# A ring of four groups of copied expert rows, and GpSimd's waits by two groups, in the expert stage of a decoder kernel

## The chip, the cores and the metric

The kernel runs on one core of a Trainium2 chip. The metric is the device time of one execution in microseconds (us); lower is better. The whole program is one launch.

## The reference

The reference is a decoder of two layers on 8 sequences of 256 tokens with 256 features, all in float32. Layer 0 has a butterfly state mixing, a cross attention on 64 context tokens and a ternary feed-forward block; layer 1 has a causal self attention, a rotary attention of 16 heads over context and sequence, and a mixture of 32 masked experts. The change lies in this last block alone:

```python
def _L1_ffn_ref(x, weight, scale, expert_masks, router_w):
    logits = jnp.einsum('bsd,ed->bse', x, router_w)
    probs = jax.nn.softmax(logits, axis=-1)
    top1_w = jnp.max(probs, axis=-1)
    top1_idx = jnp.argmax(probs, axis=-1)
    w_scaled = jnp.clip(jnp.round(weight / 0.5), -1.0, 1.0) * scale[:, None]
    def body(out, inputs):
        e_idx, mask_e = inputs
        y = jnp.einsum('bsi,oi->bso', x, w_scaled * mask_e)
        sel = (top1_idx == e_idx)[..., None]
        return jnp.where(sel, y * top1_w[..., None], out), None
...
x = x + _L1_ffn_ref(_layernorm(x, axis=-1), ...)
```

Each token goes through one expert, a 256x256 matrix of ternary values under the expert's mask.

## The kernel before

The kernel writes its waits and the order of every engine's instructions by hand: each engine has one block of code, and semaphores join them. The expert stage is the last one, after the rotary attention.

Tokens are sorted by expert. GpSimd scatters the rows of all 2048 tokens to `tokens_dram`, by 16 indirect DMAs (L1406), so that each tile of 32 rows (`HT`) holds tokens of one expert. There are 96 tiles in 12 groups (`GROUPS`) of 8 tiles (`QT`); two times 128 rows make one group, and `t` counts these halves. For each group u:

- SyncE loads its 256 rows into `sIN`, a ring of eight (`HELD`), at L1214. The load of group u waits, from u = 8 on, until group u - 8 has been stored.
- ScalarE normalizes the rows (`normal`, L1846, two instructions), and after TensorE has transposed them (L2496, four transposes) copies the transposed rows out of PSUM (`turned`, L1855) into `sXT`.
- The rows of the eight experts that the group needs are copied, from the bf16 table `EW` into float32 rows in `sE`, each 128x512: five by VectorE (`staged`, L1096, a cast) and three by ScalarE (`staged`, L1868). Which expert it is comes from a register that is loaded from `f_exu`. `sE` has two buffers, for even and odd groups, in the space of the weights `wq` and `wo`, which are no longer needed. The copy for group u waits on `f_y` until TensorE is through group u - 2.
- TensorE multiplies (`apply`, 32 matmuls in L1887), group u after the transposes of group u + 1 in its order.
- VectorE scales each half by the token's weight and the experts' scale (`scaled`, L1104) and adds the token's own row (`summed`, L1112, for group 0 by halves; `summed_both`, L1119, for the others) into `sY`, a ring of four (`RING`). `summed_both` waits until the store of group u - 4 has landed.
- GpSimd stores each half to `out` by one indirect DMA (L1431), which scatters the rows to the tokens' places.

VectorE's and ScalarE's order in the stage is fixed as follows. VectorE: copies of groups 0 and 1, the two halves of group 0 scaled and summed, copies of group 2, and then for each u from 1 on: scale u, copies of u + 2, sum u. ScalarE: copies of groups 0 and 1, `normal(0)`, `turned(0)`, `normal(1)`, and then for each u from 0 on: `turned(u + 1)`, `normal(u + 2)`, copies of u + 2. TensorE: transposes of u, then `apply(u - 1)`. GpSimd's order is the groups', and it waits once for each group (for group 0 once for each half).

Of the kernel before, what the change touches and what calls it, by code (L numbers as in the profile page):

```python
# [5 lines left out]
B, S, D = 8, 256, 256  # L6
P = 128
J, C = S // P, D // P
# [17 lines left out]
HS = P // HT  # L26
QT = 2 * HS
EARLY = 5
RING = 4
GROUPS = 12  # L30
# [16 lines left out]
def decoder_kernel(nc, I, out, rows, results):  # L47
    F32, BF, U8, U32 = mybir.dt.float32, mybir.dt.bfloat16, mybir.dt.uint8, mybir.dt.uint32
    ALU, ACT, AX = mybir.AluOpType, mybir.ActivationFunctionType, mybir.AxisListType
    ds = bass.ds  # L50

    with ExitStack() as ctx:
# [82 lines left out]
        def cut(at, shape, dt=F32, src=arena):  # L135
            n = 1
            for s in shape:
                n *= s
            words = n if dt == F32 else n // 2
            v = src[:, at:at + words]  # L140
            if dt != F32:
                v = v.bitcast(dt)
            if len(shape) > 1:
                names = "abcd"[:len(shape)]
                v = v.rearrange(f"p ({' '.join(names)}) -> p {' '.join(names)}",
                                **dict(zip(names[1:], shape[1:])))
            return v
# [64 lines left out]
        def held(eng, s, value):  # L212

            eng.wait_ge(s, value)
            eng.sem_inc(s_held, 1)
# [69 lines left out]
        def after(eng, s, value):  # L285

            if type(value) is not int or value > 0:
# [68 lines left out]

        sIN = cut(0, (HELD, 2, DW)); sXN = cut(4160, (RING, 2, D))
        sXT = cut(0, (RING, 2 * C * P), F32, early2)
        sE = [cut(0, (QT, C * D), F32, wide) for wide in (wq[:, :, :].rearrange("p c n -> p (c n)"),
                                                           wo[:, :, :].rearrange("p h d -> p (h d)"))]  # L360
        sT = cut(0, (RING, 2, D), F32, early); sY = cut(2048, (RING, 2, D), F32, early)
        fSLOT = cut(7232, (TOK, NE)); tilesB = cut(7744, (P,)); past = cut(7872, (TILES,)); fBASE = cut(7968, (2, NE))
        fNEWER = cut(8032, (J, NE)); fSHIFT = cut(8096, (NE,)); past2 = cut(8128, (TILES,)); tilesB2 = cut(8224, (P,))
# [27 lines left out]
        def _(dve):  # L391
# [697 lines left out]
            def staged(u):  # L1089

                dve.load(registers, f_exu[0:1, QT * u:QT * u + EARLY])
                if u >= 2:
                    held(dve, f_y, 2 * (u - 1))
                for t in range(EARLY):
                    expert = bass.RuntimeValue.of_register_unchecked(registers[t], min_val=0, max_val=NE - 1)
                    last = dve.tensor_copy(sE[u % 2][:, t, :], EW[:, ds(expert, 1), :].rearrange("p a n -> p (a n)"))  # L1096
                last.then_inc(f_ev, 1)

            def scaled(u, t):
# [18 lines left out]
                dve.wait_ge(f_sc, 2 * u + 2)  # L1118
                dve.tensor_tensor(sY[:, k], sT[:, k], sIN[:, u % HELD, :, 0:D], ALU.add).then_inc(f_yo, 2)  # L1119

            staged(0)
            staged(1)
            for t in range(2):
                scaled(0, t)
                summed(0, t)
            staged(2)
            for u in range(1, GROUPS):
                for t in range(2):
                    scaled(u, t)
                if u + 2 < GROUPS:  # L1130
                    staged(u + 2)
                summed_both(u)


# [82 lines left out]
        def _(pool):  # L1217
# [207 lines left out]
            for u in range(GROUPS):  # L1425
                k = u % RING
                for t in range(2):
                    if u == 0 or t == 0:
                        pool.wait_ge(f_yo, t + 1 if u == 0 else 2 * u + 2)
                    to = sIN[:, u % HELD, t, ID:ID + 1].bitcast(U32)  # L1430
                    pool.indirect_dma_start(out_rows[:, :], bass.IndirectOffsetOnAxis(ap=to, axis=0), sY[:, k, t, :], None,  # L1431
                                            bounds_check=B * S - 1, oob_is_err=False).then_inc(s_stored[k], 16)
# [5 lines left out]
        def _(act):  # L1438
# [422 lines left out]
            def staged(u):  # L1861

                act.load(registers, f_exu[0:1, QT * u + EARLY:QT * u + QT])
                if u >= 2:
                    held(act, f_y, 2 * (u - 1))
                for t in range(EARLY, QT):
                    expert = bass.RuntimeValue.of_register_unchecked(registers[t - EARLY], min_val=0, max_val=NE - 1)
                    last = act.activation(sE[u % 2][:, t, :], EW[:, ds(expert, 1), :].rearrange("p a n -> p (a n)"), ACT.Copy)  # L1868
                last.then_inc(f_ea, 1)

            staged(0)
            staged(1)
            normal(0)
            turned(0)
            normal(1)
            for u in range(GROUPS):
                if u + 1 < GROUPS:
                    turned(u + 1)
                if u + 2 < GROUPS:
                    normal(u + 2)  # L1880
                    staged(u + 2)


        @block.tensor
        def _(pe):
# [588 lines left out]
            def apply(u):  # L2474

                k = u % RING
                after(pe, f_sc, 2 if u == RING - 1 else 2 * (u - RING + 1))
                pe.wait_ge(f_ev, u + 1)
                pe.wait_ge(f_ea, u + 1)
                pe.wait_ge(f_xt, u + 1)  # L2480
                for t in range(2):
                    for c in range(C):
                        for h in range(HS):
                            first = (C * t + c) * P + h * HT
                            last = product(PS[h * HT:(h + 1) * HT, result_bank(u, t), t * D:(t + 1) * D], sXT[:, k, first:first + HT],
                                           sE[u % 2][:, HS * t + h, c * D:(c + 1) * D], c == 0, c == C - 1)
                    last.then_inc(f_y, 1)

            for u in range(GROUPS + 1):
# [64 lines left out]
```

## Time and profile before

| | us |
|---|---|
| median of 3 runs | 1120.06 |
| lowest and highest of them | 1119.53, 1125.9 |
| the profiled execution's own time | 1122.36 |
| its span, from first to last instruction | 1119.6 |
| mean granted TensorE clock over the span | 0.954 |

The span is what the profile's positions count in: a position of 1100 means 1100 us after the first instruction. The expert stage's copies begin at 1059.87 of it, so that the stage takes the last 60 us. The profiled execution's time is 2.76 us over its span. In the rows, PE is TensorE, DVE VectorE, ACT ScalarE, POOL GpSimd, SP SyncE; a q behind the name is the engine's queue, where DMAs are issued. A row of the timeline gives start, duration, engine, line, operation, what is written and read, and in square brackets how long the engine had been idle before it and what ended this.

### The profile page before, as it was taken

Reading aid. Unit: us, or ns where it says so; the run is one execution under the profiler, and the core shown is the slowest. Engines: PE = TensorE matmul, PEld = TensorE weight load, DVE = VectorE, ACT = ScalarE, POOL = GpSimd, SP = SyncE. Lnnn points to the kernel's source line nnn. Section 1 sums busy time; section 2 is a strip of 40 time slices with the busy share of each in tenths; the row PEclk is TensorE's granted clock in tenths of the full one; section 3 lists DMA queues with packets and bytes.
Section 4 is the critical chain, followed back from the end, with each engine's and each line's share of the span. In section 5 each row is a group of like instructions: output and inputs, shape, how many; then the busy total and the mean of one; then the engine's idle time right before and its main releaser. Section 6 shows DMA issues by size and latency. Waiting matters only on the chain.

```text
span 1119.6 us, 21113 instructions
## 1 busy us (share of the span) xinstructions
PE 992.0 (89%) x5879; PEld 679.0 (61%) x5887; DVE 829.7 (74%) x2532; ACT 687.0 (61%) x2310; POOL 314.5 (28%) x516
## 2 busy tenths in 40 slices
PE   7888896899999769899999999999999999968474
PEld 5674454576766435566767767667677676745342
DVE  5768875788888758878878878887788788753365
ACT  2678884776767626656665675576556756741283
POOL 3334322222223312223223222222332222101546
PEclk9789999999999979999999999999999999998687
DMA  9801002212111004000000000000000000000631
GB/s 272 296 1 38 1 0 58 58 58 56 56 56 58 19 1 129 1 16 1 1 15 1 1 16 1 15 2 1 15 1 1 15 0 6 10 1 5 233 118 63
DMA packets 36379, 47.45 MB, mean 42 GB/s; under 512 B 4659, under 2 KB 27067, under 8 KB 36032
## 3 DMA queue, kind: packets, MB, share of 16 engines
q1 hardware_dynamic: 34048, 42.04, 12.5%
q0 software_dynamic: 1920, 4.23, 1.0%
q8 instruction: 34, 0.56, 0.2%
q14 instruction: 57, 0.47, 0.1%
q10 hardware_dynamic: 320, 0.15, 0.0%
HBM read 31.65 MB, written 12.66 MB: 40 GB/s over the span
## 4 chain that ended last, share of the span: by engine, by line
PE 47%; ACT 4%; issue 3%; POOL 3%; DVE 1%; DMA 0%; ACTq 0%; POOLq 0%; DVEq 0%
PE PS L1887 40%; PE PS L2287 3%; PE PS L2267 2%; POOL out_dram L1431 2%; ACT arena L1727 1%; POOL tokens_dram L1406 1%; ACT arena L1735 1%; PE PS L2141 1%; PE PS L2289 0%; ACT causal L1759 0%; PE PS L2496 0%; ACT early L1648 0%; DMA arena<-tokens_dram 0%; PE PS L1897 0%; PE PS L2332 0%
## 5 line engine op out<-in xcount | busy, mean ns | idle before, releaser
L1887 PE MATMUL PS<-early,arena 128*32 128x128 f32 (+6 forms) x920 | 114.5, 353 | 25.0 <-DVE early L711 11.2
L1887 PE MATMUL PS<-wo,early 128*128 128x256 f32 (+1 forms) x704 | 127.7, 385 | 7.8 <-DVE sinT L912 6.4
L1343 POOL TENSOR_SCALAR small<-small 128x4 f32<-128x4 f32 x64 | 17.4, 272 | 409.9 <-ACT mask L1711 236.2
L1887 PE MATMUL PS<-EW,arena 128*128 128x256 f32 (+7 forms) x512 | 116.8, 351 | 11.3 <-DVE small L861 8.4
L1887 PE MATMUL PS<-wq,EW 128*128 128x512 f32 x256 | 124.2, 608 | 1.8 <-DVE arena L837 1.8
L1887 PEld LDWEIGHTS PS<-wo,early 128*128 128x128 f32 (+1 forms) x704 | 105.0, 171 | 32.6 <-issue 9.6
L1727 ACT ACTIVATE arena<-arena,small 128x128 f32<-128x128 f32 (+3 forms) x256 | 119.7, 480 | 4.1 <-DVE small L866 4.1
L1718 ACT ACTIVATE arena<-PS 128x512 f32<-128x512 f32 x64 | 38.6, 603 | 123.8 <-PE PS L2267 123.8
L1887 PEld LDWEIGHTS PS<-EW,arena 128*128 128x128 f32 x512 | 84.2, 192 | 41.9 <-issue 33.2
L861 DVE CUSTOM_DVE_ANT_0 arena<-PS,kmask 128x128 f32<-128x128 f32 (+3 forms) x256 | 91.6, 388 | 22.2 <-PE PS L1887 16.5
L1887 PEld LDWEIGHTS PS<-early,arena 128*32 128x32 f32 (+4 forms) x928 | 58.9, 118 | 74.7 <-issue 34.0
L1711 ACT ACTIVATE mask<-PS 128x128 f32<-128x128 f32 x256 | 67.3, 284 | 45.5 <-PE PS L1887 45.3
L789 DVE TENSOR_REDUCE small<-PS 128x2 f32<-128x256 f32 (+1 forms) x128 | 62.3, 548 | 34.3 <-PE PS L1887 33.5
L1887 PEld LDWEIGHTS PS<-wq,EW 128*128 128x128 f32 x256 | 46.1, 194 | 48.7 <-issue 46.0
L873 DVE TENSOR_SCALAR arena<-arena,small 128x128 f32<-128x128 f32 (+3 forms) x256 | 68.8, 332 | 2.3
L1345 POOL TENSOR_TENSOR small<-small,halves 128x4 f32<-128x4 f32 x64 | 67.3, 1052 | 5.3
L1743 ACT ACTIVATE early<-PS 128x512 f32<-128x512 f32 x64 | 38.1, 595 | 48.7 <-PE PS L1887 48.7
L1887 PE MATMUL PS<-arena,EW 128*128 128x512 f32 (+1 forms) x160 | 64.8, 520 | 2.5 <-ACT arena L1735 2.5
L1691 ACT ACTIVATE arena<-PS,small 128x256 f32<-128x256 f32 x128 | 62.6, 489 | 0.0
L1641 ACT ACTIVATE early<-PS 128x384 f32<-128x384 f32 x64 | 28.0, 488 | 53.1 <-PE PS L2168 53.1
L1735 ACT ACTIVATE arena<-PS 128x512 f32<-128x512 f32 x96 | 54.0, 600 | 5.6 <-PE PS L2289 3.6
L1711 ACT ACTIVATION_READ_ACCUMULATOR mask<-PS 128x1 f32 x256 | 55.2, 216 | 0.0
(341 smaller groups left out, 2316.0 us busy)
## 6 DMA issues: line engine op xcount, KB each, us to landing
EW<-in_masksT_dram SPq DMA_DIRECT2D x32, 256.0 KB, 3.5
experts_dram<-EW SPq DMA_DIRECT2D x32, 128.0 KB, 3.3
EW<-experts_dram SPq DMA_DIRECT2D x4, 1024.0 KB, 10.8
tokens_dram<-EW SPq DMA_DIRECT2D x1, 3120.0 KB, 12.9
arena<-tokens_dram SPq DMA_DIRECT2D x12, 260.0 KB, 4.2
X<-in_x_dram SPq DMA_DIRECT2D x8, 256.0 KB, 4.6
wq<-in_wq_dram SPq DMA_DIRECT2D x1, 2048.0 KB, 10.0
wo<-in_wo_dram SPq DMA_DIRECT2D x1, 2048.0 KB, 17.0
```

What stands on the lines that cost most here:

```text
L789: last = dve.tensor_reduce(d_neg[:, i % 2, j, r:r + 2], PS[:, r:r + 2, at:at + n], AX.X, ALU.max, negate=True)
L861: dve.tensor_tensor_reduce(probs(i, t), PS[:, 3 + t % 2, 0:n], kmask[:, at:at + n], 1.0, LOWEST, ALU.add, ALU.max, e_max[:, t:t + 1]).then ...
L873: last = dve.tensor_scalar(probs(i, t), probs(i, t), e_inv[:, t:t + 1], None, ALU.mult)
L1345: pool.tensor_tensor(e_rqs[:, i % 2, :], e_q3[:, i % 2, :], halves[:, 0:GH], ALU.pow).then_inc(e_rq, 1)
L1691: act.activation(dP[:, i % 2, r, P:3 * P], PS[:, r, P:3 * P], ACT.Exp, bias=d_neg[:, i % 2, 1, r:r + 1], accum_out=d_sum[:, m, 1, r, e:e + ...
L1711: last = act.activation(eSQ[:, h * XD:(h + 1) * XD], PS[:, 1, h * XD:(h + 1) * XD], ACT.Square, accum_out=e_q2[:, i % 2, h:h + 1])
L1718: act.activation(eQT.rearrange("p (t h q) -> p h t q", t=4, h=GH), PS[:, 2, :].rearrange("p (h t q) -> p h t q", t=4, h=GH), ACT.Copy).the ...
L1727: last = act.activation(tile, tile, ACT.Exp, bias=e_neg[:, i % 2, t:t + 1], accum_out=e_sum[:, i % 2, t:t + 1])
L1735: last = act.activation(ePT[:, 512 * k:512 * k + 512], PS[:, 5 + k, :], ACT.Copy)
L1743: act.activation(eOT[:, GH * g:GH * g + GH, j * P:(j + 1) * P].rearrange("p h (t q) -> p h t q", t=4), PS[:, 0, :].rearrange("p (t h q) -> ...
L1887: return pe.matmul(dst, lhs, rhs, start=first, stop=last)
L2287: pe.transpose(PS[:, 5 + k, t * P:(t + 1) * P], eP[:, i % 4, at:at + P], ident[:, :])
```

## The change

`sE` gets four buffers in the place of two. Each is now a list of eight rows of 512 floats, which may lie apart: buffers 0 and 1 lie in `wq` and `wo` as before, buffer 2 in `wk`, `wv`, `wkc`, `wvc`, buffer 3 in `w_in`, `w_out` and the upper half of `early2`; all of these are dead in this stage. The copies for group u wait for group u - 4 instead of u - 2.

Both copying engines copy groups 0 to 3 before anything else of the stage. VectorE then does for each u from 1 on: copies of u + 3, scale u, sum u. ScalarE does for u = 0: `turned(1)`, `normal(2)`; and from u = 1 on: `turned(u + 1)`, `normal(u + 2)`, copies of u + 3.

GpSimd no longer waits for each group: before group 2 it waits for the sums of groups 2 and 3, before group 4 for 4 and 5, and so on to 8 and 9. Groups 0 (by halves), 1, 10 and 11 have waits of their own.

```diff
-        sE = [cut(0, (QT, C * D), F32, wide) for wide in (wq[:, :, :].rearrange("p c n -> p (c n)"),
-                                                           wo[:, :, :].rearrange("p h d -> p (h d)"))]
+        flat = [w[:, :, :].rearrange("p a n -> p (a n)") for w in (wq, wo, wk, wv, wkc, wvc, w_in, w_out)] + [early2]
+
+        def rows_in(*parts):
+            return [cut(at + C * D * n, (C * D,), F32, flat[w]) for w, at, many in parts for n in range(many)]
+
+        sE = [rows_in((0, 0, QT)), rows_in((1, 0, QT)), rows_in((2, 0, 2), (3, 0, 2), (4, 0, 2), (5, 0, 2)),
+              rows_in((6, 0, 3), (7, 0, 1), (8, 2048, 4))]
...
             def staged(u):
-                if u >= 2:
-                    held(dve, f_y, 2 * (u - 1))
+                if u >= RING:
+                    held(dve, f_y, 2 * (u - RING + 1))
...
-            staged(0)
-            staged(1)
+            for u in range(RING):
+                staged(u)
             for t in range(2):
                 scaled(0, t)
                 summed(0, t)
-            staged(2)
             for u in range(1, GROUPS):
+                if u - 1 + RING < GROUPS:
+                    staged(u - 1 + RING)
                 for t in range(2):
                     scaled(u, t)
-                if u + 2 < GROUPS:
-                    staged(u + 2)
                 summed_both(u)
...
                 for t in range(2):
-                    if u == 0 or t == 0:
-                        pool.wait_ge(f_yo, t + 1 if u == 0 else 2 * u + 2)
+                    if u == 0:
+                        pool.wait_ge(f_yo, t + 1)
+                    elif t == 0 and u in (1, GROUPS - 2, GROUPS - 1):
+                        pool.wait_ge(f_yo, 2 * u + 2)
+                    elif t == 0 and u % 2 == 0:
+                        pool.wait_ge(f_yo, 2 * u + 4)
...
-            staged(0)
-            staged(1)
+            for u in range(RING):
+                staged(u)
             normal(0)
             turned(0)
             normal(1)
...
                 if u + 2 < GROUPS:
                     normal(u + 2)
-                    staged(u + 2)
+                if u >= 1 and u - 1 + RING < GROUPS:
+                    staged(u - 1 + RING)
```

The wait in ScalarE's `staged` and the index `u % RING` in place of `u % 2` in the copies and in `apply` change in the same way.

## Rows read from the trace of the kernel before

**Rows 1.** Windows by stretch: busy us (x instructions) of each engine, TensorE's granted clock, DMA.

```profile
core 0: us, PE busy (x) PEld busy (x) DVE busy (x) ACT busy (x) POOL busy (x), PEclk, DMA share, GB/s
...
1060.00:1070.00 10.00, 2.89 (x16) 1.83 (x20) 3.33 (x10) 6.38 (x13) 0.00 (x0) 0.50 0.71 225
...
1090.00:1100.00 10.00, 8.44 (x126) 4.34 (x116) 10.00 (x27) 10.00 (x21) 8.17 (x7) 1.00 0.42 124
...
1110.00:1120.00 10.00, 0.00 (x0) 0.00 (x0) 0.00 (x0) 0.00 (x0) 3.76 (x4) 0.50 0.03 6
```

**Rows 2.** The chain of work that ended last, its last part: start, us, what.

```profile
1079.78 2.33 POOL out_dram L1431
...
1113.69 0.98 POOL out_dram L1431
```

**Rows 3.** Timeline, all engines, beginning of the expert stage.

```profile
1059.87 1.67 ACT L1868 ACTIVATE wq<-EW 128x512 f32 x3 [8.72 <-issue]
1059.89 1.77 DVE L1096 CAST wq<-EW 128x512 f32 x5 [3.18 <-issue]
...
1061.45 1.66 ACT L1868 ACTIVATE wo<-EW 128x512 f32 x3
1061.57 1.76 DVE L1096 CAST wo<-EW 128x512 f32 x5
1064.30 1.09 ACT L1846 ACTIVATE arena<-arena 128x256 f32<-128x256 f32 x2 [1.20 <-DMA arena<-tokens_dram]
...
1069.27 3.64 PE L1887 MATMUL PS<-wq,early 128*32 128x256 f32 x32
...
1071.28 0.48 DVE L1104 SCALAR_TENSOR_TENSOR early<-PS,arena,esc 128x256 f32<-128x256 f32 x1 [7.95 <-PE PS L1887]
...
1073.07 1.67 ACT L1868 ACTIVATE wq<-EW 128x512 f32 x3 [2.12 <-PE PS L1887]
...
1073.83 1.93 PE L1887 MATMUL PS<-wo,early 128*32 128x256 f32 x32
1073.84 1.82 DVE L1096 CAST wq<-EW 128x512 f32 x5
```

**Rows 4.** Timeline, ScalarE and VectorE, steady part and end.

```profile
1077.67 0.58 ACT L1855 ACTIVATE early<-PS 128x512 f32<-128x512 f32 x1
...
1078.29 0.69 DVE L1119 TENSOR_TENSOR early<-early,arena 128x512 f32<-128x512 f32 x1
...
1079.68 1.76 DVE L1096 CAST wq<-EW 128x512 f32 x5
...
1081.36 0.69 DVE L1119 TENSOR_TENSOR early<-early,arena 128x512 f32<-128x512 f32 x1
...
1098.82 0.60 ACT L1855 ACTIVATE early<-PS 128x512 f32<-128x512 f32 x1
...
1103.48 0.67 DVE L1119 TENSOR_TENSOR early<-early,arena 128x512 f32<-128x512 f32 x1
...
1106.68 0.69 DVE L1119 TENSOR_TENSOR early<-early,arena 128x512 f32<-128x512 f32 x1
```

**Rows 5.** Timeline of GpSimd's stores.

```profile
1074.73 1.12 POOL L1431 DMA_INDIRECT out_dram<-early,arena  x1 [0.66 <-issue]
1079.78 3.12 POOL L1431 DMA_INDIRECT out_dram<-early,arena  x1 [3.93 <-DVE early L1119]
1083.20 1.15 POOL L1431 DMA_INDIRECT out_dram<-early,arena  x1 [0.30 <-issue]
...
1103.61 1.40 POOL L1431 DMA_INDIRECT out_dram<-early,arena  x1 [0.30 <-issue]
1105.31 1.31 POOL L1431 DMA_INDIRECT out_dram<-early,arena  x1 [0.30 <-issue]
...
1108.54 0.98 POOL L1431 DMA_INDIRECT out_dram<-early,arena  x1 [0.30 <-issue]
```

**Rows 6.** GpSimd's store line: time from issue to landing.

```profile
DMA to landing us min/median/max: 2.1/2.7/4.5
```

More of the change, by code:

```diff
@@ L1091, in staged @@
                 dve.load(registers, f_exu[0:1, QT * u:QT * u + EARLY])
-                if u >= 2:
-                    held(dve, f_y, 2 * (u - 1))
+                if u >= RING:
+                    held(dve, f_y, 2 * (u - RING + 1))
                 for t in range(EARLY):
                     expert = bass.RuntimeValue.of_register_unchecked(registers[t], min_val=0, max_val=NE - 1)
-                    last = dve.tensor_copy(sE[u % 2][:, t, :], EW[:, ds(expert, 1), :].rearrange("p a n -> p (a n)"))
+                    last = dve.tensor_copy(sE[u % RING][t], EW[:, ds(expert, 1), :].rearrange("p a n -> p (a n)"))
                 last.then_inc(f_ev, 1)
@@ L1863, in staged @@
                 act.load(registers, f_exu[0:1, QT * u + EARLY:QT * u + QT])
-                if u >= 2:
-                    held(act, f_y, 2 * (u - 1))
+                if u >= RING:
+                    held(act, f_y, 2 * (u - RING + 1))
                 for t in range(EARLY, QT):
                     expert = bass.RuntimeValue.of_register_unchecked(registers[t - EARLY], min_val=0, max_val=NE - 1)
-                    last = act.activation(sE[u % 2][:, t, :], EW[:, ds(expert, 1), :].rearrange("p a n -> p (a n)"), ACT.Copy)
+                    last = act.activation(sE[u % RING][t], EW[:, ds(expert, 1), :].rearrange("p a n -> p (a n)"), ACT.Copy)
                 last.then_inc(f_ea, 1)
-            staged(0)
-            staged(1)
+            for u in range(RING):
+                staged(u)
             normal(0)
@@ L2485, in apply @@
                             last = product(PS[h * HT:(h + 1) * HT, result_bank(u, t), t * D:(t + 1) * D], sXT[:, k, first:first + HT],
-                                           sE[u % 2][:, HS * t + h, c * D:(c + 1) * D], c == 0, c == C - 1)
+                                           sE[u % RING][HS * t + h][:, c * D:(c + 1) * D], c == 0, c == C - 1)
                     last.then_inc(f_y, 1)
```

## The prediction

> **What bounds the kernel now.** Start with the windows, because they tell which engines have no slack while the stage runs. Between 1090 and 1100 us VectorE and ScalarE are busy for all 10 us, TensorE for 8.44 and GpSimd for 8.17; in the last 10 us only GpSimd has any work, four instructions [rows 1]. So two engines are full in the middle, and a third one ends the program. Then the chain of work that ended last: from the store at 1079.78 to the one at 1113.69 it never leaves GpSimd [rows 2]. It is the tail that counts, and the timeline tells how it comes about. The last sum ends at 1106.68 + 0.69 = 1107.37 [rows 4], the last store instruction at 1113.69 + 0.98 = 1114.67 [rows 2], the span at 1119.6. GpSimd is 7.3 us behind VectorE when VectorE is done, and the remaining 4.93 us are the landing of the last store (2.7 us in the median [rows 6]) and the closing of the program, which the change doesn't touch.
>
> Now the pace of each engine. ScalarE: eight groups' turn, `turned(3)` at 1077.67 to `turned(10)` at 1098.82, are seven periods, 21.15 / 7 = 3.02 us [rows 4]. VectorE: 1081.36 - 1078.29 = 3.07 while GpSimd stands still, and (1103.48 - 1081.36) / 7 = 3.16 later [rows 4]. GpSimd alone: the store at 1108.54 takes 0.98 and every gap is 0.30 [rows 5]; so (1113.69 - 1108.54) / 4 = 1.29 a store, 2.58 a group [rows 2, 5]. Under VectorE it is slower: a store begun at 1103.61, 0.13 us into a sum that runs from 1103.48 to 1104.15, takes 1.40, that is 0.42 more [rows 4, 5]; 1083.20, between casts, takes 1.15, 0.17 more [rows 5]. 2.58 + 0.42 + 0.17 = 3.17, just VectorE's period. GpSimd is thus locked to VectorE at a lag, though it could go faster: the store of group 8 starts (1103.61) when the sum of group 9 starts (1103.48), and eight stores are then left.
>
> **The change part by part.**
>
> *Two more groups copied at the start, VectorE.* Two groups take 3.4 us (1059.89 to about 1063.3) [rows 3]. Two more end at about 1066.7. VectorE had been idle for 7.95 us before its first result at 1071.28 [rows 3], and that result comes no earlier now: cost nothing. If this cover were gone, it would be 3.4 us on the path.
>
> *The same on ScalarE.* Here the cover is short. One group of three copies takes 1061.45 - 1059.87 = 1.58 in start to start; two take about 3.24, to 1063.11; then ScalarE waits 1.20 us for the loaded rows and starts `normal(0)` at 1064.30 [rows 3]. With two more groups it is there at about 1066.35: 3.24 - 1.20 = +2.05 us. Everything of the head hangs on `normal(0)`: transposes, `turned(0)`, `normal(1)`, the transposes of group 1, `apply(0)`. `apply(0)` moves from 1069.27 to 1071.32, the first result from 1071.28 to 1073.33, `apply(1)` from 1073.83 to 1075.88. This presumes that TensorE's clock comes back later by as much: before, its granted clock is 0.50 between 1060 and 1070 (1.2 GHz), and the 32 matmuls of `apply(0)` take 3.64 us against 1.93 of `apply(1)` [rows 1, 3].
>
> *What the two groups give back on ScalarE.* Before, ScalarE waited 2.12 us for `apply(0)` and then copied group 2 from 1073.07 [rows 3]. Now there is nothing to copy there; it waits for the transposes of group 2, which come behind `apply(0)` and end as `apply(1)` starts, so `turned(2)` is at about 1075.95. From there each turn has the same three parts, 3.02 us: `turned(u + 1)` stands at 1075.95 + 3.02 (u - 1), and `turned(10)` at 1100.1 against 1098.82: +1.3, less than 2.05. But the last copies stand one turn earlier (u = 8 instead of 9), so that `normal(11)` is followed by nothing but `turned(11)`. `apply(9)` needs the transposes of group 10, thus `normal(10)` at the end of turn 8's second part: 1097.1 + 1.65 = 1098.7, and with 0.6 of transposes it starts at 1099.4 and ends by 1101.3. `apply(10)` (1102.4) and `apply(11)` (1104.35 to 1106.3) end the chain of products.
>
> *VectorE's order.* The same work, 3.07 to 3.16 a group. The sum of group 1 waited for products at 1075.83 before; now group 4's casts fit between, and scale(1) starts when `apply(1)` ends at 1075.88 + 1.93 = 1077.8. 0.87 of scaling and 0.69 of sum, overlapped by 0.1 as before, give the sum's end at 1079.3, against 1078.98. Seven turns on, sum(8) ends at 1079.3 + 7 x 3.07 to 3.16 = 1100.8 to 1101.4. From group 9 on there are no casts, and a group takes 1.6: sum(9) ends at 1102.4 to 1103.0. By ScalarE's and TensorE's chain (`apply(9)` over at 1101.3) it is 1102.8. I take 1102.9. Before, sum(9) ended at 1103.48 + 0.67 = 1104.15 [rows 4]. The last sum comes out at about 1107.4, as before: the gain of two copies less behind the start pays the delay of the head, and no more.
>
> *GpSimd's waits.* A wait that is already met costs nothing: gaps are 0.30 us with and without one [rows 5]. What the pairing costs is time between a sum and its store. Behind the wait stand four stores, and behind these VectorE's `summed_both` (it needs the store of four groups earlier) and SyncE's loads (they need the store of eight earlier). Group 2 waits for sum(3) at about 1085.6; the store starts 0.80 later (before, a sum over at 1078.98 and a store at 1079.78 [rows 4, 5]). Four stores at 1.29 with one to three disturbances of 0.17 to 0.42 take 5.3 to 6.2 us; the next pair comes every 6.3. So groups 2 to 7 are in step or 0.5 behind, and group 8 starts when sum(9) is done plus 0.8: 1103.7, at most 1104.6. Eight stores are left, exactly as many as before from 1103.61. 7 x 1.29 + 0.98 = 10.0, and two of 0.33 (1105.31 took 1.31 against 0.98 [rows 5]) while the last sums run: the last ends at 1114.4, at most 1115.3, against 1114.67. The landings behind it: stores of group 7 land at about 1104.9 + 2.7 = 1107.6 in the late case, and sum(11) may wait 0.9 for them; its store isn't due before 1112. The load of group 11 waits for group 3's store (about 1094.3) and is needed at 1100.6. Both are covered; without the cover of GpSimd's queue the first would cost 0.9.
>
> *The new buffers.* Same size and type of copies, same matmuls; addresses alone change. No row shows the new places; nearest are copies to `wq` and `wo`, alike at 1.76 to 1.77 and 1.67 [rows 3]. I take nothing; bounds -0.5 to +0.5 us.
>
> **Sum.** Profiled execution: 1122.36 (span 1119.6 and 2.76 around it) + 1114.4 - 1114.67 = 1122.1. The median stands 2.3 below the profiled one, 1120.06 - 0.3 = 1119.8.
>
> **The lock of the port, a rule that speaks against the change.** How long a store is held up by casts is the least certain price. The store begun at 1079.78, 0.10 us after five casts had started (1079.68), took 3.12: +2.14 [rows 4, 5]. The first 2.33 us of it, to 1082.11, which the chain counts as one piece [rows 2], end with the sum behind those casts (1081.36 + 0.69 = 1082.05). The one at 1074.73, 0.89 after casts started at 1073.84, took 1.12: +0.14 [rows 3, 5]. In the new order casts follow straight behind a sum, so that a store released by it starts 0.8 into the casts. That is the position of the second row, and I take it. The Trainium skill ("SBUF — State Buffer", Who interferes with whom) says that VectorE in a mode that uses both ports, which casts can enter, and GpSimd exclude one another for the whole instruction. By this rule the pairing would set the first of every four stores against the casts. The first row agrees with it, the rows of 0.14 and 0.17 show that a store slips in between casts.
>
> **The rivals.**
>
> *A: GpSimd is held up in each pair (slower).* If the first store of a pair loses 2.14 as at 1079.78, and the others 0.17 to 0.42, four take 5.16 + 2.14 + 0.6 = 7.9, more than the 6.3 in which two groups come. Starts are then 1086.4, 1094.3, 1102.2, 1110.1 for group 8, which is 6.5 late; the eight stores run undisturbed, as VectorE is done, and end at 1120.1: +5.4, a time of 1125.5. It decides from a pair time over 6.3. Against it: just one store in 24 shows this loss. Halfway it gives 1122.5.
>
> *B: GpSimd falls out of the lock (faster).* In bursts, no store starts just inside a sum; group 8 starts at 0.8 behind an early sum(9) (1102.4), and its eight stores lose nothing: 1103.2 + 10.0 = 1113.2, -1.5, a time of 1118.6. It can't be more: the wait for sum(9) is ahead of eight stores. For it: GpSimd needs 2.58 a group against 3.16. Against it: VectorE has work until 1107.
>
> *C: the ring does nothing and the head's 2.05 us stay.* If ScalarE's work is all that counts and turn 1 starts late by 2.05, sum(9) ends at 1104.15 + 2.05 - 1.6 (no casts) and everything is about 1 to 2 us late: 1121 to 1122.
>
> **Chances.** Forecast (1119 to 1120.9): 0.45. A: 0.2. B: 0.15. C: 0.2. The range reaches from 1117.4 (B and the noise of 0.5 in the runs, and a buffer's 0.5) to 1125.3 (nearly all of A). A measurement of this kernel can tell about 1%, 11.2 us, from no change; none of the cases reaches that, in a stage of 60 us: faster by more 0.02, within 0.94, slower by more 0.04.
>
> **What would show it.** In the new profile: `normal(0)` at about 1066.35 with no wait for the DMA; VectorE's four groups of casts done by 1067; `turned(2)` at 1075.95; sum(9) ending near 1102.9; a store starting 0.8 behind it or up to 0.9 later; the last store instruction ending at 1114.4. A shows in stores of over 2 us at the head of pairs, B in 0.98 for all and gaps at the pair's wait. I am wrong if `normal(0)` isn't late (another engine's copies held the start), if a copy at the new places takes longer, or if VectorE waits for a store to land.

## The result

| | before | changed |
|---|---|---|
| median, us | 1120.06 (13 runs) | 1127.37 (13 runs) |
| lowest and highest | 1116.34, 1125.9 | 1124.17, 1135.38 |
| ratio, with its 95% interval | | 1.0062 (1.0043 to 1.0082) |
| profiled execution: time, span | 1122.36, 1119.6 | 1135.38, 1133.4 |

The change costs 7.3 us, 0.6%. (In the four later series that have both kernels the medians are 3.1 to 3.5 us apart.) The profiled execution of the changed kernel is the longest of its 13. 6.0 us of its excess lie ahead of the expert stage: the first copy is at 1065.87 and not at 1059.87 [rows 3]. In the other profiles of the same kernel it is at 1056.74 to 1059.63, so this part doesn't belong to the change. I therefore count from each profile's first copy by ScalarE, and call the time from there to the end of the span the stage. It was 59.8 us and is 67.5.

A window of the changed kernel, 6 us later than the one from 1090 to 1100 in [rows 1], so that both lie 30.1 to 40.1 us behind the first copy:

```profile
core 0: us, PE busy (x) PEld busy (x) DVE busy (x) ACT busy (x) POOL busy (x), PEclk, DMA share, GB/s
1096.00:1106.00 10.00, 8.18 (x97) 3.65 (x89) 7.68 (x20) 6.86 (x14) 5.95 (x6) 1.00 0.39 116
```

VectorE and ScalarE, full for all of this stretch before, are busy for 7.68 and 6.86 us of it now, and 97 matmuls fall into the 10 us in place of 126 at the same granted clock (1.00, that is 2.4 GHz). No engine is full any more. The timeline tells who waits; first the beginning, against [rows 3]:

```profile
1072.12 1.08 ACT L1854 ACTIVATE arena<-arena 128x256 f32<-128x256 f32 x2
...
1077.08 3.64 PE L1896 MATMUL PS<-wq,early 128*32 128x256 f32 x32
...
1079.08 0.48 DVE L1109 SCALAR_TENSOR_TENSOR early<-PS,arena,esc 128x256 f32<-128x256 f32 x1 [6.45 <-PE PS L1896]
...
1081.46 0.60 ACT L1863 ACTIVATE early<-PS 128x512 f32<-128x512 f32 x1 [2.71 <-PE PS L2505]
```

`normal(0)` stands 6.25 us behind the first copy (before, 4.43), with no wait for the loaded rows: the head is 1.8 us longer. Now the end, all engines:

```profile
1095.19 0.66 PE L2505 MATMUL PS<-ident,arena 128*128 128x128 f32 x4 [0.50 <-ACT arena L1854]
...
1098.76 0.60 ACT L1863 ACTIVATE early<-PS 128x512 f32<-128x512 f32 x1 [2.06 <-remote]
...
1115.45 1.12 PE L1896 MATMUL PS<-early 128*32 128x256 f32 x16
...
1116.59 0.69 DVE L1124 TENSOR_TENSOR early<-early,arena 128x512 f32<-128x512 f32 x1
...
1123.63 0.88 DVE L1109 SCALAR_TENSOR_TENSOR early<-PS,arena,esc 128x256 f32<-128x256 f32 x2 [6.35 <-remote]
```

This is the finding. By TensorE's rows the last 16 matmuls are over at 1115.45 + 1.12 = 1116.57. VectorE waits for nothing but the completion of these matmuls and starts at 1123.63, 7.1 us later. ScalarE gets the transposes that end at 1095.85 at 1098.76, 2.9 us later. "remote" is what the view writes where a semaphore rose at a time at which none of its writers ended. Before, a result was taken up at once: `scaled` at 1071.28 behind the matmuls, and its wait ends with the name of its writer [rows 3]. GpSimd, against [rows 5]:

```profile
1092.92 1.07 POOL L1439 DMA_INDIRECT out_dram<-early,arena  x1 [4.16 <-DVE early L1124]
1094.29 0.98 POOL L1439 DMA_INDIRECT out_dram<-early,arena  x1 [0.30 <-issue]
1095.58 1.02 POOL L1439 DMA_INDIRECT out_dram<-early,arena  x1 [0.30 <-issue]
1096.91 1.13 POOL L1439 DMA_INDIRECT out_dram<-early,arena  x1 [0.30 <-issue]
...
1114.93 0.98 POOL L1439 DMA_INDIRECT out_dram<-early,arena  x1 [1.18 <-issue]
...
1121.38 0.98 POOL L1439 DMA_INDIRECT out_dram<-early,arena  x1 [0.30 <-issue]
1126.12 0.98 POOL L1439 DMA_INDIRECT out_dram<-early,arena  x1 [3.76 <-DVE early L1124]
```

A pair of groups is four stores without a pause, 1.3 us from start to start. Both late completions come just behind such a run: 1098.76 behind the run that ends at 1098.04, 1123.63 behind the six stores that end at 1122.36.

### The profile page after: what moved, and what is told of

Read it like the earlier page. It is cut to its first block, busy times and chain, and to the rows that moved or that the text cites. A ratio compares the mean times of both kernels' runs of the same rounds, so it can differ in the third digit from the quotient of the medians.

```text
span 1133.4 us, 21109 instructions
## 1 busy us (share of the span) xinstructions
PE 995.0 (88%) x5879; PEld 680.8 (60%) x5887; DVE 830.1 (73%) x2532; ACT 687.4 (61%) x2310; POOL 308.4 (27%) x516
## 4 chain that ended last, share of the span: by engine, by line
PE 47%; ACT 6%; issue 2%; DVE 2%; another core or an unknown queue 1%; POOL 0%; ACTq 0%; DVEq 0%; POOLq 0%
PE PS L1896 39%; PE PS L2296 3%; PE PS L2276 2%; ACT arena L1735 1%; ACT arena L1743 1%; ACT arena L1854 1%; PE PS L2150 1%; PE PS L2298 0%; ACT causal L1767 0%; ACT wq L1876 0%; PE PS L2505 0%; ACT early L1863 0%; ACT wo L1876 0%; PE PS L2341 0%
## 5 line engine op out<-in xcount | busy, mean ns | idle before, releaser
L1896 PE MATMUL PS<-wo,early 128*128 128x256 f32 (+1 forms) x608 | 121.8, 385 | 7.1 <-DVE sinT L917 6.4
L1896 PEld LDWEIGHTS PS<-wo,early 128*128 128x128 f32 (+1 forms) x608 | 101.8, 180 | 29.7 <-issue 8.3
L1896 PEld LDWEIGHTS PS<-early,arena 128*32 128x32 f32 (+4 forms) x928 | 58.1, 117 | 74.3 <-issue 34.5
L1719 ACT ACTIVATE mask<-PS 128x128 f32<-128x128 f32 x256 | 67.3, 284 | 45.2 <-PE PS L1896 44.9
L794 DVE TENSOR_REDUCE small<-PS 128x2 f32<-128x256 f32 (+1 forms) x128 | 62.3, 547 | 37.1 <-PE PS L1896 36.1
L1896 PEld LDWEIGHTS PS<-wq,EW 128*128 128x128 f32 x256 | 45.7, 193 | 48.4 <-issue 45.7
L1719 ACT ACTIVATION_READ_ACCUMULATOR mask<-PS 128x1 f32 x256 | 55.2, 216 | 0.0
```

The source lines that it names most:

```text
L794: last = dve.tensor_reduce(d_neg[:, i % 2, j, r:r + 2], PS[:, r:r + 2, at:at + n], AX.X, ALU.max, negate=True)
L1719: last = act.activation(eSQ[:, h * XD:(h + 1) * XD], PS[:, 1, h * XD:(h + 1) * XD], ACT.Square, accum_out=e_q2[:, i % 2, h:h + 1])
L1896: return pe.matmul(dst, lhs, rhs, start=first, stop=last)
```

## The experiments

The measure for all: positions in us behind the first copy, from each kernel's timeline. "Late" is whether, in the trace of the stage, a semaphore of TensorE's transposes or products rose more than 1 us after the end of the matmul that writes it. Kernels of one series ran on one chip, with the kernel before timed between them, and each of the five series on another chip; series are apart by lines. Times are of 8 to 12 executions of a kernel, the trace is of one of them.

| run | group 8's first store | last sum ends | last store ends | stage | late | ratio to before (95%) |
|---|---|---|---|---|---|---|
| before | 43.7 | 47.5 | 54.8 | 59.8 | no | |
| changed | 49.1 | 59.5 | 62.5 | 67.5 | yes | 1.0062 (1.0043 to 1.0082) |
| | | | | | | |
| control_after | 49.1 | 59.5 | 62.6 | 67.6 | yes | 1.0013 (0.9989 to 1.0037) |
| ring_only | 43.5 | 52.6 | 55.6 | 60.6 | yes | 0.9978 (0.9956 to 1.0000) |
| pairs_only | 50.0 | 51.9 | 60.5 | 65.5 | yes | 0.9998 (0.9972 to 1.0023) |
| ring_head_kept | 39.8 | 50.4 | 53.4 | 58.4 | yes | 0.9961 (0.9933 to 0.9988) |
| | | | | | | |
| pairs_paced | 45.7 | 47.4 | 57.4 | 62.3 | no | 1.0025 (0.9998 to 1.0052) |
| tail_held | 48.1 | 47.3 | 58.1 | 63.1 | no | 1.0037 (1.0014 to 1.0061) |
| stores_by_sync | | 46.8 | | 51.2 | no | 0.9935 (0.9908 to 0.9963) |
| head_kept_tail_paced | 40.2 | 44.7 | 51.4 | 56.4 | no | 0.9979 (0.9955 to 1.0002) |
| | | | | | | |
| before_again | 45.1 | 51.3 | 56.0 | 61.0 | yes | 0.9989 (0.9968 to 1.0010) |
| after_again | 48.4 | 51.5 | 58.8 | 63.7 | yes | 1.0030 (1.0001 to 1.0059) |
| pairs_again | 48.5 | 50.9 | 58.5 | 63.5 | yes | 1.0033 (1.0011 to 1.0055) |
| ring_again | 43.2 | 49.2 | 53.3 | 58.2 | yes | 0.9973 (0.9949 to 0.9997) |
| | | | | | | |
| before_third | 44.5 | 51.2 | 55.9 | 60.9 | yes | 1.0003 (0.9981 to 1.0026) |
| after_third | 47.8 | 55.2 | 58.3 | 63.2 | yes | 1.0031 (1.0012 to 1.0049) |
| last_pair_split | 47.2 | 57.4 | 60.9 | 65.8 | yes | 1.0061 (1.0038 to 1.0085) |
| best_again | 40.4 | 45.2 | 51.9 | 56.9 | yes | 0.9974 (0.9951 to 0.9996) |
| | | | | | | |
| after_fourth | 48.0 | 57.7 | 60.8 | 65.8 | yes | 1.0049 (1.0026 to 1.0073) |
| paced_again | 46.5 | 54.3 | 58.1 | 63.1 | yes | 1.0020 (1.0006 to 1.0034) |

**First series: the two halves of the change, each alone.** control_after is the changed kernel again.

> The changed kernel again, as the measure for the others on the same chip. Both theories: about 7 us over the kernel before. Theory 1 (bursts): since GpSimd now issues four to eight stores back to back, 1.29 us apart, TensorE's completions reach the other engines late in these bursts, and the profile shows semaphore updates of TensorE 2 us or more after the end of the matmul that makes them. Theory 2 (ring): the longer head on ScalarE and the new order cost, and the profile shows the same gaps wherever GpSimd's stores lie.

ring_only takes GpSimd's old waits back:

```diff
-                    if u == 0:
-                        pool.wait_ge(f_yo, t + 1)
-                    elif t == 0 and u in (1, GROUPS - 2, GROUPS - 1):
-                        pool.wait_ge(f_yo, 2 * u + 2)
-                    elif t == 0 and u % 2 == 0:
-                        pool.wait_ge(f_yo, 2 * u + 4)
+                    if u == 0 or t == 0:
+                        pool.wait_ge(f_yo, t + 1 if u == 0 else 2 * u + 2)
```

> The ring of four and the new order of copies stay, GpSimd waits for every group as before. Theory 1 (bursts of stores): most of the loss goes, the time is within 2 us of the kernel before, and late completions of TensorE are rare. Theory 2 (ring and head): the loss of 7 us stays, 1126 to 1128 us. My own sum for the ring was +0 to +2 us.

pairs_only is the kernel before with the same lines the other way round.

> Two buffers and the old order of copies, only GpSimd waits for two groups at a time. Theory 1 (bursts of stores): 5 to 8 us over the kernel before, with late completions of TensorE during bursts. Theory 2 (ring and head): within 1 us of the kernel before.

ring_head_kept is ring_only with ScalarE's copies of groups 2 and 3 moved:

```diff
-            for u in range(RING):
-                staged(u)
+            staged(0)
+            staged(1)
             normal(0)
             turned(0)
             normal(1)
...
                     normal(u + 2)
-                if u >= 1 and u - 1 + RING < GROUPS:
+                if u == 0:
+                    staged(2)
+                    staged(3)
+                elif u - 1 + RING < GROUPS:
                     staged(u - 1 + RING)
```

> As ring_only, but ScalarE copies groups 2 and 3 only after turned(1) and normal(2), so that normal(0) starts as early as before. Both theories leave the size of the head open: if the 2.05 us that I predicted for it are on the path, this is 1 to 2 us faster than ring_only and at or below the kernel before; if GpSimd's tail decides alone, the same as ring_only within 0.5 us.

Medians 1125.95, 1122.53, 1125.74 and 1118.42 us, the kernel before 1122.63 over 35 runs. The changed kernel is 3.3 us over the kernel before and not about 7, pairs_only 3.1 and not 5 to 8, and the intervals of both ratios include 1. By the medians the loss follows the pairs, not the ring, which speaks against theory 2; the third series bears it out with intervals that lie apart. Theory 1 is not clean either, since ring_only has late completions too, of 5 us at its end, though it stores in runs of two for most of the stage. The head seems to be on the path: in ring_head_kept the first result of the products is scaled 10.1 us behind the first copy, in ring_only 13.2 (in the kernel before 11.4), the stage is 2.2 us shorter and the median 4.1 us lower. The two intervals overlap, so the size of it isn't sharp.

**Second series: pauses, and other issuers.** pairs_paced has a small addition ahead of each store, head_kept_tail_paced for groups 8 to 10 alone:

```diff
+                    if 1 <= u <= 11:
+                        n = 4 * u + 2 * t
+                        pool.tensor_scalar(kmask[:, n:n + 2], mMV[:, :, 1], LN_EPS, None, ALU.add)
                     to = sIN[:, u % HELD, t, ID:ID + 1].bitcast(U32)
```

> The changed kernel with GpSimd's waits by pairs, but ahead of every store from group 1 on GpSimd does one 128x2 addition that nobody reads, so that stores start about 1.6 us apart in place of 1.29. Theory 1 (TensorE's completions are held up by unbroken runs of stores): the completions come on time, or late by less than 1 us, the last sum ends at about 1112 on the changed kernel's scale in place of 1118, and in spite of 22 times 0.3 us more of GpSimd's work the time is 1 to 4 us under the changed kernel. Theory 2 (the ring's places or order delay TensorE): completions stay late and the time rises by 2 to 4 us.

> The version with the ring, ScalarE's early head and a wait for every group, and in addition the small addition ahead of the stores of groups 8 to 10. Theory 1: the last completion, 5.4 us late there, comes on time, the last sum ends about 5 us earlier, the last store about 2 us earlier: 1 to 3 us under the version without it. Theory 2: six additions of 0.3 us on GpSimd's tail make it 1 to 2 us slower.

tail_held:

```diff
-                    elif t == 0 and u in (1, GROUPS - 2, GROUPS - 1):
+                    elif t == 0 and u == 8:
+                        pool.wait_ge(f_yo, 2 * GROUPS)
+                    elif t == 0 and u == 1:
                         pool.wait_ge(f_yo, 2 * u + 2)
-                    elif t == 0 and u % 2 == 0:
+                    elif t == 0 and u in (2, 4, 6):
                         pool.wait_ge(f_yo, 2 * u + 4)
```

> The changed kernel, but GpSimd waits for the last sum before it stores group 8, so that no store runs while TensorE has its last groups. Theory 1: the last completion comes within 1 us of the last matmul in place of 7, the last sum ends some 6 us earlier, and then eight stores follow: the time is that of the changed kernel within 2 us. Theory 2: the last completion is as late as before and the eight stores come on top, 6 to 10 us over the changed kernel.

stores_by_sync leaves out the scatter of the rows to the tokens' places; SyncE's loads of groups 8 to 11 stand between its stores:

```diff
-                    pool.indirect_dma_start(out_rows[:, :], bass.IndirectOffsetOnAxis(ap=to, axis=0), sY[:, k, t, :], None,
-                                            bounds_check=B * S - 1, oob_is_err=False).then_inc(s_stored[k], 16)
+                    at = (2 * u + t) * P
+                    to = out_rows[at:at + P, :] if u < HELD else results[at:at + P, :]
+                    sp.dma_start(to, sY[:, u % RING, t, :]).then_inc(s_stored[u % RING], 16)
```

> The changed kernel, but SyncE issues the 24 stores, by the same waits, as plain DMAs to fixed rows; what is left out is the scatter of the rows to the tokens' places, and the rows of groups 8 to 11 go to a scratch tensor. It tells whether GpSimd's instructions or the written data hold TensorE's completions up. If GpSimd's: completions on time, the last sum at 1111 to 1112 on the changed kernel's scale, and 8 to 12 us under the changed kernel, since eight stores issued by GpSimd at 1.29 us fall away behind it. If the data: completions late as before, the last sum at 1118.

Here nothing was late in any of the four, not even in tail_held, whose stores of groups 1 to 7 are the changed kernel's, in the same runs. Its last matmul, the completion taken up, and the last sum:

```profile
1105.62 1.05 PE L1898 MATMUL PS<-early 128*32 128x256 f32 x16
1106.04 0.69 DVE L1124 TENSOR_TENSOR early<-early,arena 128x512 f32<-128x512 f32 x1
1106.73 0.88 DVE L1109 SCALAR_TENSOR_TENSOR early<-PS,arena,esc 128x256 f32<-128x256 f32 x2
1108.31 0.69 DVE L1124 TENSOR_TENSOR early<-early,arena 128x512 f32<-128x512 f32 x1 [0.70 <-DMA out_dram<-early,arena]
```

The matmuls end at 1106.67, VectorE starts at 1106.73. (The last sum then waits 0.70 us for a store to land, the wait that my sum had put at 0.9.) Two of these kernels, pairs_paced and head_kept_tail_paced, ran again in later series and had late completions there: what decides whether there are any is something that differs between the series, not the kernel. So none of the four tells a thing about theory 1: a miss, since neither of the two known kernels was there as a witness. What the series does give is the changed kernel's undisturbed course: sum(9) ends 43.4 us behind the first copy in tail_held. It also shows the price of the queue of stores alone: with plain stores from SyncE the stage ends 4.3 us after the last sum, with eight stores of GpSimd behind it 15.8.

**Third series: the kernel before and the three others under one condition.** Kernels unchanged from the first series.

> The kernel before, for its profile beside the others on one chip. In four profiles taken together TensorE's completions came up to 7 us late, in the next four, taken together, not at all. If the lateness belongs to the place or the execution and not to the kernel, this profile shows it exactly when the three others of this call do. If it belongs to GpSimd's stores that aren't held by VectorE, this profile is free of it and the others have it. Expert stage, from the first copy to the end of the span: 60 us without lateness.

> The changed kernel on this chip. Theory 1 (lateness is real and belongs to the stores): late completions in the profile, expert stage 67 us. Theory 3 (lateness belongs to the execution): with no lateness the stage takes 62 to 63 us, 2 to 3 us over the kernel before, from GpSimd's waits by pairs alone; with it 67 us.

> Two buffers, waits by pairs. With lateness 65 us of expert stage as in its first profile; without, by my own sum, sum(9) stands at 1104.15 on the scale of the kernel before, eight stores start at 1105 and end at 1115 to 1116: 61 us.

> Ring of four, waits group by group. With lateness 60.6 us of expert stage as in its first profile; without it GpSimd keeps up with VectorE, the last sum stands 47.4 us after the first copy, two stores and the closing follow: 57 us, 3 us under the kernel before.

The kernel before has late completions too, by up to 3.4 us, and GpSimd then isn't locked to VectorE: of its stores several take 0.98 to 1.13 us where [rows 5] have 1.15 to 1.40. The stage is just 1.2 us longer than in the profile without lateness. The three others came out shorter than expected for late completions: 63.7, 63.5 and 58.2 us for 67, 65 and 60.6. What a late completion does to TensorE, there:

```profile
1087.75 0.88 DVE L1104 SCALAR_TENSOR_TENSOR early<-PS,arena,esc 128x256 f32<-128x256 f32 x2 [1.33 <-remote]
```

```profile
1091.02 0.66 PE L2496 MATMUL PS<-ident,arena 128*128 128x128 f32 x4 [1.93 <-ACT arena L1846]
1091.61 3.61 PE L1887 MATMUL PS<-wo,early 128*32 128x256 f32 x32
```

32 matmuls take 3.61 us there against 1.93 in [rows 3]. The windows tell why:

```profile
core 0: us, PE busy (x) PEld busy (x) DVE busy (x) ACT busy (x) POOL busy (x), PEclk, DMA share, GB/s
1086.00:1091.60 5.60, 3.22 (x40) 1.89 (x40) 3.77 (x9) 3.53 (x7) 3.78 (x4) 1.00 0.50 155
1091.60:1095.20 3.60, 3.60 (x34) 1.53 (x33) 3.50 (x8) 3.13 (x6) 2.12 (x2) 0.53 0.44 142
1095.20:1100.00 4.80, 3.94 (x57) 2.27 (x60) 4.36 (x12) 4.21 (x9) 2.86 (x3) 1.00 0.14 47
```

TensorE was busy for 3.22 us of 5.60, held up by the late completions, and then was granted 0.53: 1.2 GHz for nearly all of the stretch, and 2.4 GHz again behind it. In this trace the gap is thus paid twice. In pairs_again the clock falls in the same way between 1094.0 and 1097.4, in before_third between 1092.7 and 1096.1; in the changed kernel's own five profiles it comes to 1.00 between 13 and 16 us behind the first copy and stays there until TensorE is done, so there lateness acts by itself.

The lateness isn't tied to the expert stage. In the 28 us ahead of the first copy GpSimd scatters the rows to `tokens_dram`, the last twelve indirect DMAs 1.27 us apart, in code that the change doesn't touch. One product of TensorE in this stretch and VectorE's instruction that reads it, first in control_after, then in the profile of the kernel before that is free of lateness:

```profile
1054.77 0.63 PE L1896 MATMUL PS<-arena,ones 32*128 32x96 f32 x2
1057.95 0.24 DVE L987 TENSOR_SCALAR small<-PS 1x96 f32<-1x96 f32 x1 [2.32 <-remote]
```

```profile
1055.26 0.63 PE L1887 MATMUL PS<-arena,ones 32*128 32x96 f32 x2
1056.23 0.24 DVE L982 TENSOR_SCALAR small<-PS 1x96 f32<-1x96 f32 x1
```

VectorE starts 2.55 us behind the end of these matmuls in the one and 0.34 us in the other. All 15 profiles marked "yes" have three or four of TensorE's completions without an update of the semaphore within 0.15 us of the matmul's end during this run of scatters, and none earlier in the span; the five marked "no" have none anywhere. So the ring and its buffers can't be what makes completions late.

In this series the medians are 1121.68 for the kernel before, 1124.83 changed, 1126.64 pairs alone, 1119.41 ring alone. The ring gives 2.3 us (ratio 0.9949 to 0.9997); the pair waits on top of it cost 5.4 (1124.83 - 1119.41), and the intervals of these two kernels lie apart. The two make the 3.1 of the whole change in this series.

**Fourth series: which wait.** last_pair_split gives groups 8 and 9 a wait each:

```diff
-                    elif t == 0 and u in (1, GROUPS - 2, GROUPS - 1):
+                    elif t == 0 and u in (1, 8, 9, GROUPS - 2, GROUPS - 1):
```

> The kernel before, for its profile on this chip. If TensorE's completions come on time in it, the three others show what they do without lateness; if late, what they do with it. Expert stage 60 us on time, 61 late.

> The changed kernel. If completions are on time in this call: sum of group 9 at 43.4 us behind the first copy, as in the two relatives that ran on time, eight stores follow, expert stage 59 to 60 us, and the time within 2 us of the kernel before: then the loss is lateness alone. If they are late: stage 63 to 68 us and 3 to 7 us over the kernel before.

> The changed kernel, but groups 8 and 9 have a wait each, so that only three pairs are left. If the loss comes from the last pair's wait (GpSimd idle for the sum of group 9 with eight stores to go): stage as with waits group by group, 57 us on time, 58 to 60 late. If it comes from the three bursts before: at most 1 us under the changed kernel.

> Ring, early head on ScalarE, waits group by group and the additions between the tail's stores, again on another chip. On time: stage 56.4 us. Late: the additions break the runs of stores, and the last completion is less than 3 us late; stage 57 to 58 us. Either way 2 to 4 us under the kernel before.

Neither expectation for last_pair_split came true: with a wait less far ahead it is no faster than the changed kernel, 1127.39 against 1124.53, with intervals of the ratios that overlap a little. Its last stores, from the view of GpSimd's timeline:

```profile
1102.19 1.07 POOL L1439 DMA_INDIRECT out_dram<-early,arena  x1 [3.18 <-DVE early L1124]
1103.57 0.98 POOL L1439 DMA_INDIRECT out_dram<-early,arena  x1 [0.30 <-issue]
...
1111.31 0.98 POOL L1439 DMA_INDIRECT out_dram<-early,arena  x1 [0.30 <-issue]
1116.26 0.98 POOL L1439 DMA_INDIRECT out_dram<-early,arena  x1 [3.97 <-DVE early L1124]
```

By starting group 8 at once behind group 7, GpSimd now has a run of eight stores (1102.19 to 1112.29) in the place of four and a pause. In it TensorE moves by a few matmuls at a time:

```profile
1107.91 1.08 PE L1896 MATMUL PS<-w_in,early 128*32 128x256 f32 x3 [0.37 <-issue]
1109.33 0.41 PE L1896 MATMUL PS<-w_in,early 128*32 128x256 f32 x2 [0.33 <-issue]
...
1110.75 0.38 PE L1896 MATMUL PS<-w_out,early 128*32 128x256 f32 x1 [0.80 <-issue]
...
1112.19 0.62 PE L1896 MATMUL PS<-w_in,early 128*32 128x256 f32 x1 [0.79 <-issue]
...
1113.61 0.59 PE L1896 MATMUL PS<-w_out,early 128*32 128x256 f32 x1 [0.37 <-issue]
1113.63 2.27 PE L1896 MATMUL PS<-early 128*32 128x256 f32 x16
```

Steps of 1.42 us from 1107.91 to 1113.61, each with idle time that no other engine ended, and the rest in one go when the run is over. Group 10's products were over at 1107.54 and scaled at 1113.77, after 6.32 us of waiting, and the last sum ended at 57.4 us. The clock:

```profile
1106.00:1113.60 7.60, 4.73 (x35) 1.28 (x26) 1.31 (x3) 0.60 (x1) 4.92 (x5) 0.87 0.22 79
1113.60:1116.00 2.40, 2.29 (x17) 0.96 (x16) 1.63 (x4) 0.00 (x0) 0.00 (x0) 0.50 0.00 0
```

The pieces begin at 2.4 GHz and it is only from 1111.7 on that 1.2 is granted, so the slow clock comes behind the pieces and doesn't make them; the last 16 matmuls' 2.27 us are its price. Here the longer run went with the longer delay. Length alone doesn't decide it: ring_again has eight stores in a row from 43.2 us on, and its last completion is 2.4 us late.

**Fifth series: pauses where completions are late.** pairs_paced again, with the changed kernel as the witness.

> The changed kernel, as the witness of whether TensorE's completions are late in this call. Late: last sum 51 to 60 us behind the first copy, stage 63 to 68 us. On time: last sum at 47 to 48, stage 59 to 60 us, and the loss against the kernel before under 2 us.

> Waits by pairs and the small addition ahead of each store from group 1 on. If completions are late in this call and the short pause between stores is what lets them through: all less than 2 us late, last sum at 47.5 to 49 us, stage 62 to 63 us. If the pause doesn't matter: last sum 51 us or later, stage over 65 us.

Between the two expectations: up to group 9 the pauses do what they should (its sum ends at 44.8 us, against 47.2 in after_fourth and 43.9 in pairs_paced without lateness), in the last run of stores (from 1102.79 on, twelve, most of them 1.45 us apart) they don't: the last matmuls end at 1109.89, VectorE starts at 1114.79, 4.9 us later, and the last sum ends at 54.3. By the profiles the pauses help in part; the medians are 1124.91 against 1126.84, with intervals that overlap a little.

**The version that is faster than both.** head_kept_tail_paced (its second run is best_again): ring, early head, a wait for every group, additions in the tail. Medians 1117.5 and 1118.63 against 1120.48 and 1121.3 of the kernel before in their series, 3.0 and 2.7 us less; the first run's interval reaches 1.0002, the second's ends at 0.9996. With late completions its last sum came 45.2 us behind the first copy, where ring_head_kept had 50.4, in another series. That the additions help in the time isn't shown: without them ring_head_kept was 4.2 us under the kernel before in its series (0.9933 to 0.9988), and the two never ran in one.

## Why the prediction was wrong

*What held.* The head: 1.8 us for forecast 2.05. VectorE's two groups of copies cost nothing: it idled 6.45 us before its first result. `turned(2)` came 15.6 us behind the first copy, forecast 16.1. Sum(9) was forecast at 1102.9 on the old scale, 43.0 behind the first copy; tail_held, undisturbed, has 43.4. Four stores of a pair take 5.1 us (1092.92 to 1098.04), forecast 5.3 to 6.2. The new buffers: four groups of casts took 6.8 us, twice the 3.4 of two.

*The step that failed* stands in the part on GpSimd's waits: "group 8 starts when sum(9) is done plus 0.8: 1103.7, at most 1104.6", and before it, in ScalarE's part, that `apply(9)` is over at 1101.3. Both take the pace from [rows 4], 3.02 to 3.16 us a group, as if it were free of what GpSimd does. In the profiles of the changed kernel sum(9) ends 47.0 to 48.3 us behind the first copy and not 43; group 8's stores start at 47.8 to 49.1 (forecast 43.8 to 44.7, the kernel before 43.7 to 45.1). Then the eight stores, which I had taken as 10.0 us without a break, are six and a wait for the last sum in four of the five profiles (3.76 us in the one above); in after_again they run through. Against the kernel before in the same series these are 3.3 us at the start of group 8's stores, and in all 2.3 to 2.7 us of stage (63.2 against 60.9, 63.7 against 61.0); in the series without a profile of the kernel before the stage reached 65.8 to 67.6. Of the 7.3 us of the first comparison the 3.1 to 3.5 of the later ones are so accounted for. The rest stays open; the two profiles, one without late completions and one with, are 7.7 us of stage apart.

*The cover that I didn't see.* I counted the wait for sum(9) in the place of sum(8) as free, because the eight stores behind it were the same eight. They are the same in number, but GpSimd's queue lost its head start. With late completions sum(9) ends as late in the kernel before (47.6 us in before_again, 47.4 in before_third) as in the changed one (47.6, 47.0); but the kernel before stores group 8 at 45.1 and 44.5, ahead of this sum, and the changed one must wait for it, until 48.4 and 47.8. In the ring with a wait per group sum(9) ends at 44.1 to 44.3 and group 8's first store is at 43.2 to 43.5, with pairs on top of the ring 5.2 to 5.6 later in the same series; so there the pairs also delay the sum itself by 3.6 to 4.0 us. My bound "at most 1104.6" came from stores alone.

*Rival A* (a store held up by casts in each pair) had the sign and nearly the size, 1125.5, but not the cause. In the changed kernel no store behind group 0 takes over 1.32 us: a store released 0.8 into the casts takes 1.07 and loses 0.09, about what the row at 1074.73 had said [rows 5]. In pairs_only, with the old order on VectorE, two stores do take 3.13, the second at the head of the pair of groups 6 and 7; group 8's first store is 2.4 us behind sum(9) there. The rule that a mode with both ports shuts GpSimd out (the Trainium skill, "SBUF — State Buffer", Who interferes with whom) was thus seen in the old order alone and isn't what made the change slow.

*Rival B*'s mechanism came true, where pairs are left out: ring_again falls out of the lock, gains 2.3 us in the median and 2.8 of stage. *Rival C* didn't.

*What stays open.* That unbroken runs of GpSimd's stores hold up TensorE's completions rests on where they lie in time, in the run of scatters ahead of the stage and in the stage, with none in the 1040 us before, and on the pieces of 1.42 us; that it happens in four series and not in a fifth is shown as well. What in the chip does it, and why one series was free of it (each had its own chip, and its own time), no run tells. Nor is it known whether GpSimd's instructions or the data that they write do it: stores_by_sync was to tell, but ran where nothing was late. Late completions are known from traces alone, one for each kernel of a series; the profiles that have them also lack an update of their own for 28 to 41 completions of VectorE and ScalarE, all from 12 us ahead of the first copy on, where those on time lack at most one. Whether recording the trace has a part in it is untested. Nor does any run tell whether the changed kernel would be no slower in a series such as the second: it didn't run there. By the undisturbed sum(9) I would estimate a stage of 59 to 60 us (43.4 + 0.8 + 10.0 to 10.7 + 4.9), equal to the kernel before.

## What to carry to other kernels

A queue of work at the end that one engine does alone is worth its head start: don't let its first item wait for a later one to save a wait that is already met. When an engine is let out of step with others, ask what its unbroken bursts do to engines that share nothing with it in the program. And one profile of the kernel before is one condition: here it showed 59.8 us for a stage that takes 61 in two others, with other gaps; have the unchanged kernel as a witness in every series.

## What the runs showed of the hardware

- TensorE's completions can reach VectorE and ScalarE up to 7.1 us after the end of the matmul in its row, while GpSimd issues indirect DMAs 1.27 to 1.45 us apart and just behind such a run (the changed kernel's profile; 2.55 us in the run of scatters of control_after). The completions of VectorE and ScalarE that have an update of their own have it within 0.02 us.
- In one such run TensorE's matmuls came in pieces, 1.42 us apart, at first at the full granted clock: a group's 32 took 8.0 us (1107.91 to 1115.90, last_pair_split) in place of 1.93.
- The clock can fall behind such gaps: 0.53 granted between 1091.60 and 1095.20 in before_again, where 32 matmuls took 3.61 us.
- In one series of four kernels, and in the first profile of the kernel before, none of this was seen, with the same runs of scatters and, in tail_held, of stores.
- The lock of the kernel before, two stores for one period of VectorE of 3.16 us, depends on where in VectorE's work a store starts: with VectorE's casts moved ahead of the scaling, most stores take 0.98 to 1.13 us.
